# Edge MLP of a message-passing stage: from 125-edge chunks on tiles of 125 nodes to visits of 128-edge pairs on tiles of 64 nodes

## The reference

```python
row, col = (edge_index[0], edge_index[1])
msg_in = jnp.concatenate([node_features[row], node_features[col], edge_features], axis=1)
h = jax.nn.relu(msg_in @ W1.T + b1)
messages = h @ W2.T + b2
agg = jax.ops.segment_sum(messages, col, num_segments=node_features.shape[0])
upd_in = jnp.concatenate([node_features, agg], axis=1)
g = jax.nn.relu(upd_in @ U1.T + c1)
return g @ U2.T + c2
```

## Time and profile before

| quantity | value |
| --- | --- |
| median of 3 runs | 3607.83 us (3603.68 to 3612.74) |
| profiled execution, its own time | 3592.89 us |
| its span | 3591.2 us |
| granted TensorE clock, mean | 0.703 of full |
| PE busy | 2767.2 us, 77% |
| PE weight loads busy (beside PE) | 1734.4 us |
| POOL busy | 1795.6 us, 50% |
| DVE busy | 1627.7 us, 45% |
| ACT busy | 999.8 us, 28% |
| DMA | 108.52 MB, mean 30 GB/s |

### The profile page before, as it was taken

The page is one execution under the profiler, slowest core; times in us unless marked ns, Lnnn a source line. Parts: engine busy times, 40 slices in busy tenths (PEclk is TensorE's granted clock), DMA queues, the critical chain, the costliest instruction groups (busy, mean ns, idle before and its releaser), DMA issues. The chain is left out here.

```text
span 3591.2 us, 51132 instructions
## 1 busy us (share of the span) xinstructions
PE 2767.2 (77%) x11270; PEld 1734.4 (48%) x11271; DVE 1627.7 (45%) x4686; ACT 999.8 (28%) x1815; POOL 1795.6 (50%) x1780
## 2 busy tenths in 40 slices
PE   3677788878999999998798899799636666666665
PEld 1233444457777777774444454354423333333333
DVE  7999222233333333332346436436524444444444
ACT  1333122221111111111110311211225454554543
POOL 2000000007777777772575475477037777777772
PEclk9999877765555555556899899899755555555556
DMA  0000000012222222221111011011021111111111
GB/s 7 3 0 0 20 0 0 0 49 55 53 53 54 55 53 53 54 54 38 31 17 12 11 17 13 10 17 17 28 87 35 35 35 35 35 35 35 35 35 32
DMA packets 181949, 108.52 MB, mean 30 GB/s; under 512 B 140291, under 2 KB 164066, under 8 KB 181148
## 3 DMA queue, kind: packets, MB, share of 16 engines
q0 software_dynamic: 88960, 66.98, 9.0%
q1 hardware_dynamic: 91662, 40.38, 4.4%
q10 hardware_dynamic: 1296, 0.79, 0.1%
HBM read 93.22 MB, written 13.33 MB: 30 GB/s over the span
## 5 line engine op out<-in xcount | busy, mean ns | idle before, releaser
L1720 POOL DMA_INDIRECT adj<-h_rows,adj x468 | 599.1, 1280 | 243.6 <-POOL adj L1716 124.9
L947 POOL DMA_INDIRECT work<-p_rows,work x468 | 569.4, 1217 | 242.8 <-POOL work L943 124.9
L1556 PE MATMUL ps<-adj,small 125*128 (+1 forms) x3150 | 631.5, 357 | 0.0
L1283 POOL DMA_INDIRECT edge_rows<-pay,small x425 | 513.6, 1208 | 129.2 <-issue 128.6
L1857 PE MATMUL ps<-adj 125*128 125x125 f32 x948 | 257.0, 442 | 313.1 <-DVE adj L1760 313.1
L1556 PEld LDWEIGHTS ps<-adj,small 125*128 125x128 bf16 x3150 | 311.5, 99 | 274.9 <-issue 12.6
L1857 PEld LDWEIGHTS ps<-adj 125*128 125x128 f32 x948 | 214.0, 326 | 399.2 <-DVE adj L1760 287.9
L1094 PE MATMUL ps<-small 64*125 64x128 f32 x936 | 337.2, 457 | 0.0
L928 POOL IOTA work<- 125x25 f32 x1 | 0.2, 154 | 656.7 <-POOLq L98 656.7
L986 DVE TENSOR_TENSOR work<-ps,work 125x384 f32<-125x384 f32 x156 | 87.1, 558 | 458.7 <-PE ps L1094 339.3
L1102 PE MATMUL ps<-work 125*128 125x125 f32 x936 | 249.3, 436 | 42.3 <-ACT work L1033 42.1
(11 more groups left out here) (318 smaller groups left out, 3727.4 us busy)
## 6 DMA issues: line engine op xcount, KB each, us to landing
small<-edge_attr SPq DMA_DIRECT2D x156, 93.8 KB
work<-p_rows,work POOLq DMA_INDIRECT x468
adj<-h_rows,adj POOLq DMA_INDIRECT x468, 3.4
edge_rows<-pay,small POOLq DMA_INDIRECT x425, 2.6
adj<-edge_rows SPq DMA_DIRECT2D x5, 996.1 KB
pay<-edge_pay SPq DMA_DIRECT2D x106, 46.9 KB
x_kept<-work SPq DMA_DIRECT2D x2, 1562.5 KB, 8.7
work<-x_kept SPq DMA_DIRECT2D x2, 1562.5 KB, 6.6
```

What stands on the lines that cost most here:

```text
L947: eng.indirect_dma_start(gathered[h][:, k * D:(k + 1) * D], None, p_rows[:, :], bass.IndirectOffsetOnAxis(ap=idx[h][:, k:k + 1], axis=0)). ...
L1283: eng.indirect_dma_start(edge_rows[:, :], bass.IndirectOffsetOnAxis(ap=place[:, k:k + 1], axis=0), pay[:, k * ROW:(k + 1) * ROW], None).th ...
L1556: ins = eng.matmul(ps[:, j, 0:cw], parts[k][:, i * D:(i + 1) * D], cols, start=first and i == 0, stop=last and i == 2, skip_group_check=True)
L1720: eng.indirect_dma_start(gathered[h][:, k * D:(k + 1) * D], None, h_rows[:, :], bass.IndirectOffsetOnAxis(ap=idx[h][:, k:k + 1], axis=0)). ...
```

## The change

`walk` goes. Edges are cut into chunks of 128, two of which form a pair (208 pairs, padded at the end); nodes into 49 tiles of 64. As edges are sorted by target, the pairs and the tiles are merged: a visit is a pair together with a tile that it may touch. There are always 208 + 49 - 1 = 256 visits, listed in order in a table `visit` (tile in the upper bits, pair in the low byte), which DVE and PE compute in the setup from the last target of each pair. Each engine runs a loop over quads of four visits, and loads the table's word for a visit into a register where it needs tile or pair.

For one visit: SP loads the targets of the pair's 256 edges, spread over 64 partitions, into the upper half of one of four buffers `kmat`, and the 64 attribute rows into the lower half. DVE turns the upper half into a one-hot by comparing with the node numbers (L1036 of the new code). The buffer is then one operand of 128 rows: PE multiplies it in one f32 matmul per chunk by `qw`, which holds for each tile 64 rows of q and below them the 64 rows of `w1e` (`w1e` is repeated for all 49 tiles in the setup). DVE builds the one-hot edge by node, 128 x 64, per chunk directly in f32 (L1041); ACT takes the relu; PE's total is a sum of two f32 matmuls on 64 columns into one of two PSUM buffers, which DVE adds to the tile's columns of R (L1061), cleared in the setup. The transposes, the bf16 parts and the widening are gone.

POOL gathers each pair once, into a ring of four pair buffers: 416 gathers, written out without a loop and without the index copy; the indices are a column of the loaded table. Before a ring slot is used again, POOL loads from the table `done` the number of adds to wait for. A pair visited for two tiles is added, relued and multiplied for each of them.

```diff
+EW, PAIR = 128, 2
+PAIRS = -(-E // (PAIR * EW))
+TP = PAIRS // 2
+MW = 64
+MT = -(-N // MW)
+VISITS = PAIRS + MT - 1
+KB, RING, LAG = 4, 4, 2
+assert PAIRS == 2 * TP and VISITS == 256 and N - (MT - 1) * MW < MW
+
...
-def walk(nc, eng, ranges, row, body, end):
...
+    quads = [(g, range(4 * g, min(MT, 4 * g + 4))) for g in reversed(range((MT + 3) // 4))]
...
+    gathered, dst_f = l_(EW, RING * PAIR * D), l_(EW, PAIR * PAIRS)
+    rows = [l_(EW, PAIR * D) for _ in range(2)]
+    kmat = [l_(128, PAIR * EW) for _ in range(KB)]
...
+    PROD = [ps[0:EW, b, 0:PAIR * D] for b in range(2)]
+    SUM = [ps[:, 4 + b, 0:MW] for b in range(2)]
...
+    def pair_of(v):
+        return nc.s_assert_within(v & 255, 0, PAIRS - 1)
+
+    def tile_of(v):
+        return nc.s_assert_within(v >> 8, 0, MT - 1)
+
+    def load_visit(eng, v):
+        at = v if isinstance(v, int) else nc.s_assert_within(v, 0, VISITS - 1)
+        return eng.value_load(visit[0:1, bass.ds(at, 1)], min_val=0, max_val=((MT - 1) << 8) + PAIRS - 1)
+
+    def quads_of(eng, body):
+
+
+        body(0, True, False)
+        with eng.Fori(1, VISITS // KB - 1) as i:
+            body(i * KB, False, False)
+        body(VISITS - KB, False, True)
...
+            eng.dma_start(dst_f.bitcast(I32), a["dst_cols_all"]).then_inc(s_dst, 16)
+            eng.wait_ge(s_count, 1)
+            eng.dma_start(qw3[FE:128, 0:HELD, :],
+                          a["mlp_w1e"].unsqueeze(1).to_broadcast([FE, HELD, D])).then_inc(s_late, 16)
+            eng.wait_ge(s_tab, 1)
+
+            def body(v0, first, end):
+                for b in range(KB):
+                    v = v0 + b
+                    g = pair_of(load_visit(eng, v))
+
+                    eng.wait_ge(s_prod, v + 1)
+                    eng.dma_start(kmat[b][0:MW, :].bitcast(I32),
+                                  a["dst_all"].rearrange("(o e) -> o e", o=1)[:, bass.ds(g * (PAIR * EW), PAIR * EW)]
+                                  .to_broadcast([MW, PAIR * EW])).then_inc(s_km[b], 16)
+                    eng.dma_start(kmat[b][MW:128, :],
+                                  a["edge_attr_64"][:, bass.ds(g * (PAIR * EW), PAIR * EW)]).then_inc(s_km[b], 16)
+
+            quads_of(eng, body)
...
+            for g in range(PAIRS + LAG):
+                if g < PAIRS:
+                    if g >= RING:
+                        n = eng.value_load(done[0:1, g - RING:g - RING + 1], min_val=1, max_val=VISITS)
+                        eng.wait_ge(s_add, nc.s_assert_within(n, 1, VISITS) + 2)
                         eng.nop(nofuse=True)
-                    eng.tensor_copy(idx[h], src_i[:, bass.ds(c + h * UH, UH)]).then_inc(s_idx[h], 1)
-                    eng.wait_ge(s_idx[h], q + 1)
+                    for k in range(PAIR):
+                        at = (g % RING * PAIR + k) * D
+                        c = g * PAIR + k
+                        eng.indirect_dma_start(gathered[:, at:at + D], None, p_rows[:, :],
+                                               bass.IndirectOffsetOnAxis(ap=src_i[:, c:c + 1], axis=0)
+                                               ).then_inc(s_g[g % RING], 16)
+                if g >= LAG:
+                    eng.wait_ge(s_g[(g - LAG) % RING], 16 * PAIR * ((g - LAG) // RING + 1))
+                    eng.nop(nofuse=True).then_inc(s_gd, 1)
...
+            for n, (g, tiles) in enumerate(quads):
+                w0, n_w, tall = tiles[0], len(tiles), min(MW, N - tiles[0] * MW)
+                eng.wait_ge(s_qrow, n + 1)
+                if w0 == 0:
+                    eng.wait_ge(s_kept, 16)
+                eng.tensor_tensor(qw3[0:tall, w0:w0 + n_w, :],
+                                  ps[0:tall, 4 + g % 4, 0:n_w * D].rearrange("p (s c) -> p s c", c=D),
+                                  b1[0:tall, :].unsqueeze(1).to_broadcast([tall, n_w, D]), ALU.add).then_inc(s_q, 1)
+            eng.wait_ge(s_dst, 16)
+            eng.tensor_copy(dst_f, dst_f.bitcast(I32)).then_inc(s_f, 1)
+            eng.wait_ge(s_prow, 16 * NGR)
+            eng.memset(R, 0.0).then_inc(s_clear, 1)
...
+            def hots(v, b, word, i):
+                g, w = pair_of(word), tile_of(word)
+                eng.wait_ge(s_km[b], i)
+                eng.nop(nofuse=True)
+                eng.tensor_scalar(kmat[b][0:MW, :], kmat[b][0:MW, :].bitcast(I32), node_id[:, bass.ds(w, 1)], None,
+                                  ALU.is_equal).then_inc(s_ht, 1)
+                eng.wait_ge(s_tot, v + 1)
+                eng.nop(nofuse=True)
+                for k in range(PAIR):
+                    ins = eng.tensor_scalar(hot[b % 2][:, k * MW:(k + 1) * MW], iota, tile_lo[:, bass.ds(w, 1)],
+                                            dst_f[:, bass.ds(g * PAIR + k, 1)], ALU.add, ALU.is_equal)
+                ins.then_inc(s_hot, 1)
+
+            def add(v, b, word):
+                g = pair_of(word)
+                eng.wait_ge(s_gd, g + 1)
+                eng.wait_ge(s_prod, v + KB + 1)
+                eng.wait_ge(s_tot, v + 1)
+                eng.nop(nofuse=True)
+                eng.tensor_tensor(rows[b % 2], PROD[b % 2],
+                                  gathered[:, bass.ds((g & (RING - 1)) * (PAIR * D), PAIR * D)],
+                                  ALU.add).then_inc(s_add, 1)
+
+            def collect(v, b, word):
+                w = tile_of(word)
+                eng.wait_ge(s_tot, v + 3)
+                eng.wait_ge(s_r, v + 2)
+                eng.nop(nofuse=True)
+                r = R[:, bass.ds(w * MW, MW)]
+                eng.tensor_tensor(r, r, SUM[b % 2], ALU.add).then_inc(s_r, 1)
+
+            def body(v0, first, end):
+                words = {0: load_visit(eng, v0)}
+                if first:
+                    hots(0, 0, words[0], 32)
+                else:
+                    words[-1] = load_visit(eng, v0 - 1)
+                for b in range(KB):
+                    v = v0 + b
+                    if b < KB - 1 or not end:
+                        words[b + 1] = load_visit(eng, v + 1)
+                        n = (v0 // KB if isinstance(v0, int) else v0 >> 2) + (b + 1) // KB
+                        hots(v + 1, (b + 1) % KB, words[b + 1], n * 32 + 32)
+                    add(v, b, words[b])
+                    if b or not first:
+                        collect(v - 1, (b - 1) % KB, words[b - 1])
+                if end:
+                    collect(VISITS - 1, KB - 1, words[KB - 1])
...
+            eng.dma_start(qw3[FE:128, HELD:MT, :],
+                          a["mlp_w1e"].unsqueeze(1).to_broadcast([FE, MT - HELD, D])).then_inc(s_w1e, 16)
...
+            def body(v0, first, end):
+                for b in range(KB):
+                    eng.wait_ge(s_add, v0 + (b + 3))
                     eng.nop(nofuse=True)
+                    eng.activation(rows[b % 2], rows[b % 2], ACT.Relu).then_inc(s_relu, 1)
...
+                for i, w in enumerate(tiles):
+                    tall = min(MW, N - w * MW)
+                    ins = eng.matmul(ps[0:tall, 4 + g % 4, i * D:(i + 1) * D], x[:, w * MW:w * MW + tall], wb,
+                                     start=True, stop=True)
+                ins.then_inc(s_qrow, 1)
...
+            def products(v, b):
+                w = tile_of(load_visit(eng, v))
+                eng.wait_ge(s_ht, v + 1)
+
+                eng.wait_ge(s_add, v + 1)
+                eng.nop(nofuse=True)
+                for k in range(PAIR):
+                    ins = eng.matmul(PROD[b % 2][:, k * D:(k + 1) * D], kmat[b][:, k * EW:(k + 1) * EW],
+                                     qw[:, bass.ds(w * D, D)], start=True, stop=True)
+                ins.then_inc(s_prod, 1)
+
+            def total(v, b):
+                eng.wait_ge(s_hot, v + 1)
+                eng.wait_ge(s_relu, v + 1)
+
+                eng.wait_ge(s_r, v + 1)
+                eng.nop(nofuse=True)
+                for k in range(PAIR):
+                    ins = eng.matmul(SUM[b % 2], rows[b % 2][:, k * D:(k + 1) * D], hot[b % 2][:, k * MW:(k + 1) * MW],
+                                     start=k == 0, stop=k == PAIR - 1)
+                ins.then_inc(s_tot, 1)
+
+            def body(v0, first, end):
+                if first:
+                    products(0, 0)
+                for b in range(KB):
+                    if b < KB - 1 or not end:
+                        products(v0 + b + 1, (b + 1) % KB)
+                    total(v0 + b, b)
...
-    deg, agg, out = T[3][0:1, :], T[1], T[1]
+    deg, agg, out = T[1][0:1, :], T[1], T[1]
```

More of the change, by code:

```diff
@@ L963, in _ @@
-            eng.wait_ge(s_dst, 1)
-            eng.wait_ge(s_q, len(groups))
-            eng.memset(zero, 0.0).then_inc(s_const, 1)
-            eng.wait_ge(s_const, 4)
-            def hots_of(w, c, q, h):
-                if not first_of_all(q):
-                    eng.wait_ge(s_tr[h], q)
-                    eng.wait_ge(s_h32[h], q)
-                for k in range(UH):
```

(33 more changed lines are left out.)

303 lines of the change are left out of this document (109 added, 194 removed).

## The result

| | before | after | ratio, 95% interval |
| --- | --- | --- | --- |
| median of 4 runs, first chip | 3607.81 us | 3704.61 us (3700.24 to 3705.30) | 1.0265 [1.0247, 1.0283] |
| profiled execution | 3592.89 us | 3704.45 us | |
| medians again, chip 8 | 3589.59 us | 3666.18 us | 1.0212 [1.0195, 1.0229] |

What follows compares the result with a forecast made beforehand. PE and gathers bound the old loop, a DVE-ACT-PE lap the new: 64 x (3 x 3.26 + 4.9) = 940 us, +96 at its end. 3592.89 + 96 = 3689, plus 15 for the median, stated as 3705; range 3600 to 3790.

Steps and rivals of the forecast that it cites:

- The mechanism: Edge loop: each visit is one full lap over DVE, ACT and PE, overlapping nothing of the next; 940 us in all.
- The sign that was named for it: Profile after: the wait of DVE's by-edge tensor_scalars would be put down to PE's total; no size given.
- rival 2: PE's part of the lap is cheaper, through hidden weight loads (3647 us) or a 2.4 GHz clock (3628); chance 0.18.
- The ordinary lap: Three of four visits per quad: 2.30 us from add to total's end plus 0.96 to the next add, 3.26 us.
- the 0.33 for filling and draining: PE's total: 0.33 us beyond four records at their pitch (0.86 us), making about 1.20 us.
- The first visit of a quad: DVE's loop branch and three word loads instead of one make this visit 4.9 us (bounds 3.3 and 5.3).
- The start: After the setup, the loop's first add comes at about 803 us instead of 807 (bounds 797 and 812).
- The sum: Edge loop: start 803 + 940 of visits + 2 for the last collect gives 1745 against 1649.4, +96 us.
- Gathers: POOL: 416 gathers at 1.51 us, 3.02 us a pair, 628 us for 208 pairs; no longer the bound.
- Rival 1: DVE's operations on the lap collide with gathers: 3730 to 3792 us, say 3765; chance 0.15.
- Rival 3: DVE's register work runs hidden under data operations: laps of 2.85 us in all visits, 3493 us; chance 0.14.
- PE and the gathers bound the loop together: Edge loop before the change: PE busy 798.51 of 842.0 us, gather half-units 830; lightening PE alone would gain nothing.

Runs made afterwards that it cites:

- half_total: Changed kernel with one of the two matmuls of each visit's total left out: 3609.85 us.
- hot4: Changed kernel with four by-edge one-hot buffers instead of two, and two kmat buffers instead of four: 3610.76 us.
- carry: Changed kernel with DVE's two repeated word loads at the start of a quad replaced by carried registers: 3588.12 us.
- open_lap: Changed kernel with four by-edge one-hot and two kmat buffers, carried words, no DVE asserts on pair and tile, setup's weights loaded first: 3474.42 us, ratio 0.9676.
- after_again: Changed kernel without any edit, measured and profiled again on chip 8: 3666.18 us, ratio 1.0212.
- before_few_gathers: Kernel before the change with two of the three gathers of each half-unit: 3509.06 us.
- reorder: Changed kernel with DVE's by-edge one-hots of the next visit, and their wait for the total, moved behind the add: 3649.33 us.
- body8: Changed kernel with loop bodies of eight visits instead of four on all engines: 3618.27 us.
- open_reorder8: Changed kernel with by-edge one-hots behind the add, carried words, no DVE asserts on pair and tile, weights loaded first, bodies of eight visits: 3371.29 us, ratio 0.9396.

## Why the prediction was right, point by point

The mechanism was right; that the predicted 3705 met 3704.61 to the microsecond was luck, in two ways. Errors of the loop's sum cancelled, as told below. And the sum was for the profiled execution, 3689, which came out at 3704.45: its 15 us more are mainly genconv's 20.8, which no term of the sum had, less 3.5 in the interaction. The 15 us that the forecast added for the median, because before's profile lay under its median, happened to match them, though after's profile lies on its median. Setup and both ends of the loop in the first profile after:

```profile
765.88 1.05 SPq L916 DMA_DIRECT2D small<-dst_all  x1
...
766.98 1.38 SPq L917 DMA_DIRECT2D small<-dst_all  x1
...
780.24 7.59 PE L1108 MATMUL ps<-small,work 128*125 128x128 f32 x50 [15.77 <-DMA small<-mlp_w1b]
...
799.46 0.68 DVE L1015 TENSOR_TENSOR work<-ps,small 64x512 f32<-64x512 f32 x1 [0.19 <-PE ps L1124]
...
801.30 2.33 SPq L930 DMA_DIRECT2D work<-dst_cols_all  x1
...
807.35 0.38 DVE L1019 CAST work<-work 128x416 f32<-128x416 int32 x1 [7.21 <-DMA work<-dst_cols_all]
807.66 1.29 POOL L975 DMA_INDIRECT work<-p_rows,small  x1 [7.86 <-DMA p_rows<-work]
...
819.31 0.42 DVE L1051 TENSOR_TENSOR work<-ps,work 128x256 f32<-128x256 f32 x1 [3.31 <-issue]
...
1744.94 0.22 DVE L1061 TENSOR_TENSOR work<-work,ps 128x64 f32 x1 [0.62 <-PE ps L1154]
```

- **The mechanism** (one lap over DVE, ACT and PE) is as forecast: shown by half_total and hot4. The sign that was named for it came only in part: of the 56.1 us that DVE idles before the by-edge one-hots the page puts most down to issue (38.2), because DVE waits only some 0.25 us a lap for the total. Behind that wait stands DVE's own sequencer, forecast under rival 2 at 2.86 us a visit and measured at 2.84.
- **The ordinary lap** was forecast at 3.26 us and is 3.09: 192 x 0.17 = 33 us too much. The total takes 1.09 for 1.20 (the pitch is that of the earlier trace rows; the 0.33 for filling and draining was too much), the hand-overs 0.09 and 0.07 for 0.10 and 0.12. From total's end to the next add it is 0.97, forecast 0.96.
- **The first visit of a quad**, forecast 4.9, is 4.99: 64 x 0.09 = 6 us too little. That the extra is the sequencer's loads is shown by carry: 1.25 us of it went with two loads.
- **The start** of the loop was forecast at 803 and is 819.31, 16 us too early. PE's products began at 780.24, not 775.07, behind two small loads issued first (765.88, 766.98); moved back in open_lap they gave 7 us (first add 42.0 us into the stage, 49.3 in hot4). The target load stands behind the writes of p_rows and the q products (801.30), and landed at 807.35; I had not counted it. The first gather left at 807.66, behind the write of p_rows. Some 4 of the 16 us are of this profile alone: the first add came 53.4 us into the stage, and 49.6 in after_again.
- **Stalls** of 0.7 us: the mean distance of adds is 3.62 here and 3.55 in after_again, 255 x 0.07 = 18 us that the forecast didn't have. The other three executions on the first chip took 3700 to 3705 us, so they probably had them too; what causes them is open.
- **The sum**: two small terms go with these. It counted 256 distances where 256 adds have 255, 5 us too much, and the laps of the last body are 3 us shorter. -33 + 6 + 16 + 18 - 5 - 3 = -1: the last collect came at 1744.94, forecast 1745. Chip 8, without the stalls, has +77 us instead of +97.
- **Gathers** were priced at 1.51 us and came at a pitch of 1.25, 2.50 us a pair instead of 3.02. They are off the lap, so it changed nothing.
- **Rival 1** (collisions on the lap) fell. The by-edge one-hots stand on the lap; here they are in after_again:

```profile
L1041 DVE TENSOR_SCALAR small<-work,small x512: 304/313/465, 816.7 to 1723.4; 128x64 f32<-128x64 f32 x171
```

  The median is 0.313 us for the 312 that ran beside a gather and for the 200 others alike, so they pay no price. The exclusive lock of the Trainium skill (SBUF — State Buffer, "SBUF: two separate sides") may have been met by single operations of 0.465 us. Off the lap there is a price: the by-node one-hots (L1036) took 0.443 us in the median of 158 beside a gather, 0.345 in the 98 others, and laps with a long one are no longer than the rest, 3.09 us. In the trace before, all 73 tensor_scalars of L975 over 0.5 us ran beside a gather, and none of the 139 that ran beside none is over 0.35.
- **Rival 2**: the clock stayed at 0.50, and four records took 1.09 us, a pitch of 0.21 as in the earlier trace rows. What a shorter total would give is bounded by half_total: 56 us. The pull-ahead of weight loads (the Trainium skill, TensorE: Matmul & The Clock Gate, "Step-by-step: what each phase is for") doesn't show as a shorter pitch here. The prediction read the pitch as load and matmul not hiding one another fully; but one total's four loads take 0.93 us beside its 1.09 us of matmuls, and starts of loads and of matmuls are both 0.21 us apart.
- **Rival 3** (register work is free) fell: it costs as counted, and was the part of the chain that could be taken away.
- **Wrong in the first part**: "PE and the gathers bound the loop together". The gathers did. The conclusion for PE's work held (worth nothing), the bound of 44 us for POOL's, set in before_few_gathers by PE's 798 busy us, did not: 80.

## What to carry to other kernels

When a change cuts the work of the busiest engines and yet lengthens the kernel, look for a lap: follow one item over the engines by start times and ask what the next item waits for in program order. Where the engine on the lap also steers the loop, count its register loads, asserts and wait values: here they cost as much as its data operations, and taking them off (two loads per body, asserts, longer bodies), with the wait moved behind the add and the setup's weight loads moved ahead (7 us), turned +2.1% into -6.0%. A busy share of 95% at a low granted clock was no bound here: take work away from each engine in turn and see.

## What the runs showed of the hardware

- PE's busy time stretched to the time there was: with 936 fewer matmuls the granted clock went from 0.55 to 0.50 and busy time in 730 us only from 696 to 664; with fewer gathers the clock went to 0.62.
- VectorE's sequencer set the pace of a loop: the durations of its records plus 0.037 us for each record on the engine came to 2.84, 2.71, 2.85 and 2.97 us a visit where 2.84, 2.71, 2.85 and 2.95 were measured (half_total twice, hot4, reorder).
- A VectorE tensor_scalar of 64 x 256 from int32 to f32 took 0.443 us beside an indirect gather and 0.345 without; one of 128 x 64 in f32 took 0.313 either way.
- A gather of 128 rows took 0.95 us on POOL where one of 125 rows took 1.21; the pitch went from 1.51 to 1.25. What makes the difference was not tested.
- Genconv, unchanged in code, took 835 to 844 us in most profiles and 853 to 858 in three (after, body8, open_reorder8), with the interaction 3 to 7 us shorter than before's 961.2 in them. Between two profiles it makes some 20 us. Its cause stays open.
